# Perceiver layer on one core: block scales on GpSimd, early residual products, products of zeros on TensorE

## The chip, the cores and the metric

The kernel is one program on one core of one Trainium2 chip (trn2). The core has TensorE (PE), VectorE (DVE), ScalarE (ACT), GpSimd (POOL) and SyncE (SP), which run side by side and wait for each other by semaphores. The metric is the device time of one execution in microseconds. PEld is TensorE's weight load, which overlaps its products; PEclk is TensorE's granted clock as a share of full speed (1.00 is 2.4 GHz, 0.50 is 1.2 GHz).

## The reference

The layer takes x (4 x 256 x 256) and a context (4 x 4096 x 256), both f32, and adds three parts to x:

```python
x = x + xattn(layernorm(x), ctx, ctx)   # q, k, v products; focus (log, softmax, x mean) of q and k;
                                        # of 16 values in each head the 11 largest kept;
                                        # kv = k^T v per head; y = q kv / (q . mean k); y @ Wp.T
x = x + attn(layernorm(x))              # q * cumsum(k * v) * sigmoid(gate), with biases
x = x + ffn(layernorm(x))               # silu(gate) * up, then down: NVFP4 fake quantization of
                                        # rows, of the hidden rows and of the three weights
```

Fake quantization: every block of 16 values gets a scale, its absolute maximum / 6 times a global scale, limited to 448 and rounded to fp8 (e4m3); the values are divided by it and rounded to fp4 (e2m1). The global scale of a weight is 448 x 6 / (absolute maximum of the whole weight); that of the rows is an input (s_in, s_in_down).

## The kernel before, in words

Rows lie on the 128 partitions, and a group is 1024 rows: eight tiles of 128 rows by 256 columns. Group 0 is the query (x), groups 1 to 16 are the context. The order of each engine is written out by hand, and each engine's queue runs in that order; `wait_ge` holds up the engine and everything behind it in its queue.

**Start.** SyncE issues the loads: x in four parts, Wk, the first context group, gate_w, up_w, down_w, Wv, Wp. ScalarE's queue issues Wq. VectorE builds `ident` (`identity`), takes the statistics of x and writes the normalised rows `x_hat` (`query_rows`, L1238). TensorE transposes Wq (`transpose_quad(0, ...)`), then the query's rows (`query_turn`, L783), and multiplies (`project`, L811: eight products of 128x256 for two tiles). ScalarE moves each quad of transposes from PSUM to SBUF (`evacuate_quad`, L429) and lifts each product (`lift`, L482). VectorE takes between them the block maxima of the three weights of the feed-forward part (`weight_max`, L1268) as they land, and the sorting keys of the query's halves (`query_keys`, L1372). ScalarE's exponentials (L516) and VectorE's reciprocal of their sums (L1290) close group 0.

**Groups 1 to 16, in pairs.** VectorE makes keys (L1280), sorts them by a network of min and max (L1305 to L1356), makes the mask (L1363), and applies it (L1296). TensorE transposes, projects (L811) and sums k^T context (L908); ScalarE lifts, takes logarithms and exponentials and scales the rows (L528). Once the block maxima are there, GpSimd reduces their maximum over the partitions (L406, at 45.7 us).

**Attention.** Behind the last group: `mix` (products of q with kv, division on VectorE, L1449 to L1453), `mixed_quad` (transposes of the mixed rows, L783), `project_out` (L896), `add_attention`, statistics; then gates, running sums and, between them, the fp4 codes of the three weights (`scale_weight`, `weight_codes`). Between mix(1) and mix(2) VectorE's queue has `weight_scales` (L1507 to L1529: all scales of the feed-forward part, block scales rounded to fp8 in `w_fp8`, and `ident_out`, the identity times 1/out_scale); `weight_reciprocals` (L1534 to L1536) comes later.

**Feed-forward.** Four chunks of two tiles. TensorE: `gate_up` (L1029), `hidden_oct` (eight transposes of a tile's codes, L1039), `down`: the residual product `ident_out` x `xs` (L1049), then eight products with `downT` (L1052). ScalarE: `silu_half` (L671), `hidden_oct` (L679, one copy of 128x1024), `finish_rows` (L685) and `finish_tile` (L691). VectorE: `hidden` (L1483) and the quantization of the hidden rows, ending in L1214 for each tile. SyncE stores.

Of the kernel before, what the change touches and what calls it, by code (L numbers as in the profile page):

```python
# [18 lines left out]
P = 128  # L19
# [12 lines left out]
T = 8  # L32
# [32 lines left out]
def perceiver_layer(nc, x, ctx, Wq, Wk, Wv, Wp, focus, W_qkv, b_qkv, W_gate, b_gate,  # L65
# [9 lines left out]
    with es:  # L75
# [5 lines left out]
        oct_bank = bank[6:8]  # L81

# [87 lines left out]
        x_hat = expo[1]  # L170

# [36 lines left out]
        ident_ready = sem("ident_ready")  # L208
        w_rest_loaded = sem("w_rest_loaded")
# [10 lines left out]
        w_max_taken = sem("w_max_taken")  # L220
        front_loaded = [sem(f"front_loaded{s}") for s in range(PER_BATCH)]
# [52 lines left out]
        ident_out_ready = sem("ident_out_ready")  # L274
        down_in_psum = sem("down_in_psum")
# [6 lines left out]
        EVERY, LOWER, UPPER = slice(0, T), slice(0, T // 2), slice(T // 2, T)  # L282
        NORM_TILES = (LOWER, UPPER, LOWER, UPPER, LOWER, UPPER)
# [96 lines left out]
        def _(pool):  # L380
# [27 lines left out]


            pool.wait_ge(small_loaded, 64)  # L410
# [7 lines left out]
        def _(act):  # L418
# [203 lines left out]
            def spread_fp8(i, dst, fp8):  # L622

                act.wait_ge(fp8_rounded, max(i - 1, 1))
# [49 lines left out]
            def hidden_oct(t):  # L674
# [4 lines left out]
                act.activation(hid_fp4T[:, t % 2, :, :], oct_bank[t % 2][:, :].bitcast(BF16).rearrange("p (k c) -> p k c", k=8),  # L679
# [96 lines left out]
        def _(pe):  # L776
# [16 lines left out]

            pe.wait_ge(ident_ready, 4)
            pe.wait_ge(wq_loaded, 16)
            transpose_quad(0, two_tiles(w_rows, 0))

# [235 lines left out]
            def hidden_oct(t):  # L1033
# [3 lines left out]
                for b in range(8):  # L1037
                    at = (t % 2) * HIDDEN + b * P
                    ins = pe.transpose(oct_bank[t % 2][:, :].bitcast(BF16)[:, b * P:(b + 1) * P],  # L1039
                                       hid_fp4[:, at:at + P], ident_b[:, :])  # L1040
                ins.then_inc(oct_in_psum, 1)

            def down(t):

                c = t // 2
                dst = (bank[4] if t == T - 1 else bank[4 + c % 2])[:, (t % 2) * D:(t % 2 + 1) * D]
                if c >= 2:
                    pe.wait_ge(rows_out_ready, c - (t < T - 1))
                pe.matmul(dst, ident_out[:, :], xs[:, t, :], start=True, stop=False)  # L1049
                pe.wait_ge(oct_in_sbuf, FFN_OCTS + 2 + t + 1)  # L1050
                for k in range(HIDDEN // P):
                    ins = pe.matmul(dst, hid_fp4T[:, t % 2, k, :], downT[:, k, :], start=False, stop=(k == HIDDEN // P - 1))  # L1052
# [58 lines left out]
        def _(dve):  # L1111
# [108 lines left out]
            def identity():  # L1220

                step(dve.memset(ident[:, :], 0.0))
# [281 lines left out]
            each = lambda a: a[:, :].rearrange("p (w o) -> p w o", o=1).broadcast_to([P, 3, P])  # L1504
            flat_w = lambda a: a[:, :, :].rearrange("p w b -> p (w b)")

            def weight_scales():  # L1507

                dve.wait_ge(small_loaded, 64)
                dve.wait_ge(absmax_reduced, 1)  # L1510
                step(dve.reciprocal(in_scale_inv[:, :], in_scale[:, :]))
                then(dve.reciprocal(w_scale[:, :], w_absmax_all[:, :]))
                step(dve.tensor_scalar(in_sixth[:, :], in_scale[:, :], 1.0 / FP4_MAX, None, ALU.mult))
                then(dve.tensor_scalar(w_scale[:, :], w_scale[:, :], FP8_MAX * FP4_MAX, None, ALU.mult))
                step(dve.tensor_scalar(in_undo[:, :], in_scale_inv[:, :], NEARLY_ONE / HALF_WAY, None, ALU.mult))
# [184 lines left out]
```

## Time and profile before

| | |
|---|---|
| median of 3 runs | 482.53 us (481.84 to 482.94) |
| the profiled execution | 481.86 us, its span 480.1 us |
| busy VectorE, TensorE, ScalarE, GpSimd | 449.7, 383.1, 361.4, 7.4 us |
| granted clock of TensorE, mean | 0.947 |

The time of an execution is a little longer than its span, the stretch from the first to the last instruction in the record. In a row of the timeline stand the start in us, the duration in us, the engine, the line of the kernel, the operation, output<-input, the shape, how many instructions are merged (x8), and in brackets how long the engine had been idle before and what ended that. The end of a product on TensorE is modelled, and a group of products of which the ends overlap shows a little more than it occupies. In the chain, each row is start, length, engine, what, line.

### The profile page before, as it was taken

Reading aid. Unit: us, or ns where it says so; the run is one execution under the profiler, and the core shown is the slowest. Engines: PE = TensorE matmul, PEld = TensorE weight load, DVE = VectorE, ACT = ScalarE, POOL = GpSimd, SP = SyncE. Lnnn points to the kernel's source line nnn. Section 1 sums busy time; section 2 is a strip of 40 time slices with the busy share of each in tenths; the row PEclk is TensorE's granted clock in tenths of the full one; section 3 lists DMA queues with packets and bytes.
Section 4 is the critical chain, followed back from the end, with each engine's and each line's share of the span. In section 5 each row is a group of like instructions: output and inputs, shape, how many; then the busy total and the mean of one; then the engine's idle time right before and its main releaser. Section 6 shows DMA issues by size and latency. Waiting matters only on the chain.

```text
span 480.1 us, 5971 instructions
## 1 busy us (share of the span) xinstructions
PE 383.1 (80%) x1877; PEld 303.2 (63%) x1880; DVE 449.7 (94%) x706; ACT 361.4 (75%) x952; POOL 7.4 (2%) x22
## 2 busy tenths in 40 slices
PE   2996649998998988997897997991999789537764
PEld 1875537787776876886786885891885445213343
DVE  6699999999999999999999999999998879899993
ACT  2469986997997987997887988976438568666764
POOL 2001000000000000000000000000000000000000
PEclk9999879999999999999999999997899999958878
DMA  7933100230220230140140140041010000000001
GB/s 232 354 115 120 55 1 1 87 89 1 88 88 1 69 107 2 50 126 1 46 131 1 42 129 6 1 127 49 13 76 0 1 2 0 1 0 1 23 22 44
DMA packets 27070, 27.65 MB, mean 58 GB/s; under 512 B 1184, under 2 KB 26784, under 8 KB 27040
## 3 DMA queue, kind: packets, MB, share of 16 engines
q1 hardware_dynamic: 26464, 27.00, 17.9%
q8 instruction: 15, 0.25, 0.2%
q10 hardware_dynamic: 416, 0.26, 0.2%
q14 instruction: 15, 0.12, 0.1%
q0 software_dynamic: 160, 0.01, 0.0%
HBM read 26.22 MB, written 1.05 MB: 57 GB/s over the span
## 4 chain that ended last, share of the span: by engine, by line
DVE 73%; PE 9%; issue 9%; ACT 7%; DMA 1%; SPq 0%; ACTq 0%
DVE focus_words L1296 8%; DVE focus_words L1280 8%; DVE sorted L1319 4%; DVE level L1305 4%; DVE level L1306 4%; DVE sorted L1320 4%; DVE merge L1332 4%; PE bank L811 4%; DVE sorted L1197 3%; DVE amax L1166 2%; DVE sorted L1325 2%; DVE sorted L1324 2%; DVE keymax L1322 2%; DVE merge L1330 2%; DVE rank L1343 1%
## 5 line engine op out<-in xcount | busy, mean ns | idle before, releaser
L811 PE MATMUL bank<-WkT,rows_T 128*128 128x256 f32 x512 | 125.2, 391 | 33.5 <-ACT rows_T L429 33.5
L811 PEld LDWEIGHTS bank<-WkT,rows_T 128*128 128x128 f32 x512 | 95.3, 194 | 50.5 <-ACT rows_T L429 39.2
L908 PE MATMUL bank<-ctx_words,focus_words 128*128 128x257 f32 x512 | 115.3, 383 | 3.5 <-ACT focus_words L528 3.5
L908 PEld LDWEIGHTS bank<-ctx_words,focus_words 128*128 128x128 f32 x512 | 99.5, 197 | 16.1 <-ACT focus_words L528 5.5
L516 ACT ACTIVATE focus_words<-focus_words,shift,ff 128x256 f32<-128x256 f32 x136 | 79.8, 590 | 0.6
L482 ACT ACTIVATE focus_words<-bank 128x256 f32<-128x256 f32 x136 | 50.2, 381 | 28.8 <-PE bank L811 28.8
L528 ACT ACTIVATE focus_words<-focus_words,row_scale 128x256 f32<-128x256 f32 x136 | 56.2, 512 | 11.6 <-DVE row_scale L1298 11.6
L429 ACT ACTIVATE rows_T<-bank 128x512 f32<-128x512 f32 x78 | 44.2, 595 | 17.5 <-PE bank L783 17.5
L783 PE MATMUL bank<-ident,ctx_words 128*128 128x128 f32 x256 | 38.2, 278 | 3.5 <-DMA ctx_words<-in_ctx_dram 2.8
L1363 DVE TENSOR_TENSOR mask<-focus_words,fifth 128x2048 bf16<-128x2048 f32 x17 | 39.0, 2292 | 0.5
L783 PEld LDWEIGHTS bank<-ident,ctx_words 128*128 128x128 f32 x256 | 31.6, 144 | 11.5 <-DMA ctx_words<-in_ctx_dram 5.2
L1296 DVE TENSOR_TENSOR focus_words<-focus_words,mask 128x2048 f32<-128x2048 f32 x17 | 38.5, 2267 | 0.0
L1280 DVE SCALAR_TENSOR_TENSOR focus_words<-focus_words,key_and,key_xor 128x2048 int32<-128x2048 int32 x16 | 37.5, 2345 | 0.0
L499 ACT ACTIVATE focus_words<-focus_words 128x2048 f32<-128x2048 f32 x17 | 32.5, 1911 | 0.0
L993 PE MATMUL bank<-WattT,rows_T 128*128 128x512 f32 x64 | 29.4, 595 | 0.0
L482 ACT ACTIVATION_READ_ACCUMULATOR focus_words<-bank 128x1 f32 x136 | 27.9, 205 | 0.0
L1029 PE MATMUL bank<-gateT,focus_words 128*128 128x512 bf16 x29 | 11.6, 481 | 18.3 <-DVE ctx_words L1483 10.1
L516 ACT ACTIVATION_READ_ACCUMULATOR focus_words<-focus_words,shift,ff 128x1 f32 x136 | 25.7, 189 | 0.0
L1319 DVE TENSOR_TENSOR sorted<-level 128x1024 f32<-128x1024 f32 x17 | 20.8, 1224 | 0.5
L783 PE MATMUL bank<-ident,focus_words 128*128 128x128 f32 x64 | 11.4, 314 | 12.4 <-DMA focus_words<-in_L_xattn_Wq_dram 4.6
L1320 DVE TENSOR_TENSOR sorted<-level 128x1024 f32<-128x1024 f32 x17 | 20.7, 1218 | 0.0
L1332 DVE TENSOR_TENSOR merge<-sorted 128x1024 f32<-128x1024 f32 x17 | 20.7, 1217 | 0.0
(198 smaller groups left out, 584.1 us busy)
## 6 DMA issues: line engine op xcount, KB each, us to landing
ctx_words<-in_ctx_dram SPq DMA_DIRECT2D x32, 512.0 KB, 4.0
ctx_words<-in_L_ffn_gate_w_dram SPq DMA_DIRECT2D x2, 1024.0 KB, 8.4
ctx_words<-in_L_ffn_up_w_dram SPq DMA_DIRECT2D x2, 1024.0 KB, 9.3
xs<-in_x_dram SPq DMA_DIRECT2D x4, 256.0 KB, 5.6
ctx_words<-in_L_ffn_down_w_dram SPq DMA_DIRECT2D x2, 512.0 KB, 9.7
ctx_words<-in_L_ffn_down_w_dram SPq DMA_DIRECT2D x1, 1024.0 KB, 4.9
out_dram<-xs SPq DMA_DIRECT2D x3, 256.0 KB, 2.1
gateT<-in_L_attn_W_qkv_dram SPq DMA_DIRECT2D x1, 512.0 KB, 6.2
```

The costliest lines, as they stand in the source:

```text
L429: ins = act.activation(dst, src, ACT.Copy, scale=scale)
L482: ins = act.activation(lifted[(s + 1) % 2][:, t, :], proj_bank[m][:, (t % 2) * D:(t % 2 + 1) * D], ACT.Prelu, bias=NOT_ZERO, alpha=-0.01, ...
L516: ins = act.activation(expo[slot][:, t, :], lifted[slot][:, t, :], ACT.Exp, bias=shift[:, t:t + 1], scale=ff[:, 0:1], accum_out=exp_sum[:, ...
L528: ins = act.activation(expo[slot][:, t, :], expo[slot][:, t, :], ACT.Identity, scale=row_scale[:, slot, t:t + 1])
L783: ins = pe.transpose(quad_bank[par][:, b * P:(b + 1) * P], src, ident[:, :])
L811: ins = pe.matmul(proj_bank[m][:, t * D:(t + 1) * D], rows_T[:, m % 2, 2 * t + k, :], WT[:, k, :], start=(k == 0), stop=(k == KT - 1))
L908: ins = pe.matmul(sum_bank[k][:, 0:GW], heads_half(expo[slot][:, t, :], k), ctx_ring[:, s, t, :], start=(s == 0 and t == 0), stop=(s == PE ...
L1280: dve.scalar_tensor_tensor(out=key[n % 2].bitcast(I32), in0=lifted[(s + 1) % 2].bitcast(I32), scalar=key_and[:, 0:1], in1=key_xor[:, :].re ...
L1296: tt(expo[slot], expo[slot], mask[:, :, :], ALU.mult).then_inc(masked_ready, 1)
L1319: step(tt(sorted4[:, :, 2:4, :], level1[:, :, 0:2, :], level1[:, :, 2:4, :], ALU.max))
L1320: step(tt(sorted4[:, :, 0:5:4, :], level1[:, :, 0:2, :], level1[:, :, 2:4, :], ALU.min))
L1332: step(tt(low[:, at], sorted4[:, :, 0:4, 0:32], sorted4[:, :, 0:4, 32:64], ALU.min))
```

## The change

Four things are changed.

1. VectorE's `weight_scales` is taken apart. The four instructions with a reciprocal (or its factor) go into `tensor_scales`, in front of group 3's sorting. The other 13, and the first two of `weight_reciprocals`, run on GpSimd behind its all-reduce, each waiting for the one before by `pstep`; `out_undo` is a product there, not a reciprocal.
2. The residual product of `down` becomes `residual(t)`. For the even tiles it comes ahead of `hidden_oct`; for the last tile it comes between the two `hidden_oct` of the last chunk.
3. The last tile's transposes go half to their old bank and half to bank 0; ScalarE copies the first half, VectorE the second.
4. VectorE clears `zero_cols` (512 bf16 columns of `mask`) first of all, and TensorE multiplies them with themselves, 8 times ahead of Wq's transposes and 10 times behind, into a bank that is used later.

```diff
+        zero_cols = mask[:, 0:2, :].rearrange("p t c -> p (t c)")
...
+            pool.wait_ge(w_scale_ready, 1)
+            pool.tensor_scalar(in_sixth[:, :], in_scale[:, :], 1.0 / FP4_MAX, None, ALU.mult).then_inc(pstep, 1)
...
+            pool.wait_ge(pstep, 7)
+            pool.tensor_scalar(ident_out[:, :], ident[:, :], out_undo[:, 0:1], None, ALU.mult).then_inc(ident_out_ready, 1)
+            pool.tensor_tensor(w_amax[:, :, :], w_amax[:, :, :], each(w_sixth), ALU.mult).then_inc(pstep, 1)
+            pool.wait_ge(pstep, 8)
+            pool.tensor_scalar(w_amax[:, :, :], w_amax[:, :, :], FP8_MAX, None, ALU.min).then_inc(pstep, 1)
+            pool.wait_ge(pstep, 9)
+            pool.tensor_scalar(flat_w(w_magic), flat_w(w_amax), FP8_MAGIC, FP8_LEAST, ALU.mult, ALU.max).then_inc(pstep, 1)
+            pool.wait_ge(pstep, 10)
+            pool.tensor_tensor(flat_w(w_amax), flat_w(w_amax), flat_w(w_magic), ALU.add).then_inc(pstep, 1)
+            pool.wait_ge(pstep, 11)
+            pool.tensor_tensor(flat_w(w_fp8), flat_w(w_amax), flat_w(w_magic), ALU.subtract).then_inc(w_fp8_ready, 1)
+            pool.wait_ge(w_fp8_ready, 1)
+            pool.tensor_tensor(w_rcp[:, :, :], w_fp8[:, :, :], each(w_undo), ALU.mult).then_inc(pstep, 1)
+            pool.wait_ge(pstep, 12)
+            pool.tensor_scalar(w_rcp[:, :, :], w_rcp[:, :, :], TINY / HALF_WAY, None, ALU.max).then_inc(w_undone, 1)
...
+            blocks = slice(0, 4 if t == T - 1 else 8)
+            act.activation(hid_fp4T[:, t % 2, blocks, :], ...
...
+            def zero_products(n):
+                for _ in range(n):
+                    pe.matmul(sum_bank[1][:, :], zero_cols[:, 0:P], zero_cols, start=True, stop=True)
+            pe.wait_ge(zeros_ready, 1)
+            zero_products(8)
             pe.wait_ge(ident_ready, 4)
             pe.wait_ge(wq_loaded, 16)
             transpose_quad(0, two_tiles(w_rows, 0))
+            zero_products(10)
...
+            def residual(t):
                 c = t // 2
                 if c >= 2:
                     pe.wait_ge(rows_out_ready, c - (t < T - 1))
+                pe.matmul(down_dst(t), ident_out[:, :], xs[:, t, :], start=True, stop=False)
...
+                more = c + 1 < CHUNKS
+                residual(2 * c)
                 hidden_oct(2 * c)
+                if not more:
+                    residual(2 * c + 1)
                 hidden_oct(2 * c + 1)
                 down(2 * c)
+                if more:
+                    residual(2 * c + 1)
                 down(2 * c + 1)
...
+                dve.memset(zero_cols, 0.0).then_inc(zeros_ready, 1)
...
+            def tensor_scales():
+                dve.wait_ge(small_loaded, 64)
+                dve.wait_ge(absmax_reduced, 1)
+                step(dve.reciprocal(in_scale_inv[:, :], in_scale[:, :]))
+                then(dve.reciprocal(w_scale[:, :], w_absmax_all[:, :]))
+                then(dve.tensor_scalar(w_scale[:, :], w_scale[:, :], FP8_MAX * FP4_MAX, None, ALU.mult))
+                dve.reciprocal(w_scale_inv[:, :], w_scale[:, :]).then_inc(w_scale_ready, 1)
...
+                if a == 3:
+                    tensor_scales()
...
             def weight_reciprocals():
-                settle()
-                then(dve.tensor_tensor(w_rcp[:, :, :], w_fp8[:, :, :], each(w_undo), ALU.mult))
-                then(dve.tensor_scalar(w_rcp[:, :, :], w_rcp[:, :, :], TINY / HALF_WAY, None, ALU.max))
+                dve.wait_ge(w_undone, 1)
                 then(dve.reciprocal(w_rcp[:, :, :], w_rcp[:, :, :]))
...
             mix(0)
             mix(1)
-            weight_scales()
             mix(2)
...
+            dve.wait_ge(oct_in_psum, FFN_OCTS + 2 + T)
+            dve.tensor_copy(hid_fp4T[:, (T - 1) % 2, 4:8, :],
+                            last_half_bank[:, :].bitcast(BF16)[:, 0:4 * P].rearrange("p (k c) -> p k c", k=4))\
+                .then_inc(last_oct_half, 1)
```

## Rows read from the trace of the kernel before

**Rows 1.** The page's part 4: the chain that ended last, by engine.
```profile
DVE 73%; PE 9%; issue 9%; ACT 7%; DMA 1%; SPq 0%; ACTq 0%
```
**Rows 2.** Waits of VectorE: us in total, times, longest us.
```profile
DVE focus_words L1490 <- ACT ctx_words L652: 4.8, 4, 2.1
...
DVE rcp_sum L1290 <- ACT focus_words L516: 0.2, 1, 0.2
```
**Rows 3.** Timeline of the start, TensorE: the query's transposes and products.
```profile
9.85 1.97 PE L783 MATMUL bank<-ident,focus_words 128*128 128x128 f32 x8 [4.18 <-DVE focus_words L1238]
...
12.53 3.78 PE L811 MATMUL bank<-WqT,rows_T 128*128 128x256 f32 x8 [0.71 <-ACT rows_T L429]
...
16.96 2.69 PE L811 MATMUL bank<-WqT,rows_T 128*128 128x256 f32 x8
...
19.93 1.89 PE L811 MATMUL bank<-WqT,rows_T 128*128 128x256 f32 x8
```
**Rows 4.** Windows: PE, PEld, DVE, ACT, POOL busy (instructions), PEclk, DMA share, GB/s.
```profile
12.00:16.00 4.00, 3.47 (x8) 2.75 (x9) 2.40 (x10) 0.97 (x2) 0.51 (x2) 1.00 1.09 348
...
423.00:424.00 1.00, 1.00 (x4) 0.39 (x3) 1.00 (x2) 0.00 (x0) 0.00 (x0) 0.50 0.00 0
...
475.00:476.00 1.00, 1.00 (x6) 0.75 (x5) 0.00 (x0) 0.00 (x0) 0.00 (x0) 0.52 0.00 0
```
**Rows 5.** Timeline of the start, ScalarE and VectorE.
```profile
11.90 1.07 ACT L429 ACTIVATE rows_T<-bank 128x512 f32<-128x512 f32 x2
...
16.19 2.29 DVE L1268 TENSOR_REDUCE w_amax<-ctx_words 128x128 f32<-128x2048 f32 x1 [1.55 <-DMA ctx_words<-in_L_ffn_gate_w_dram]
...
20.56 1.28 DVE L1372 SCALAR_TENSOR_TENSOR focus_words<-focus_words,key_and,key_xor 128x1024 int32<-128x1024 int32 x1 [2.08 <-ACT focus_words L482]
```
**Rows 6.** Timeline, TensorE: bf16 products of 128x512 in the feed-forward part.
```profile
422.24 1.03 PE L1029 MATMUL bank<-gateT,focus_words 128*128 128x512 bf16 x2 [3.27 <-DVE ctx_words L1483]
423.06 1.06 PE L1029 MATMUL bank<-upT,focus_words 128*128 128x512 bf16 x2
```
**Rows 7.** DMA issues of the first 30 us: KB, median us to landing.
```profile
ctx_words<-in_L_ffn_up_w_dram SPq DMA_DIRECT2D x1, 1024.0 KB, 13.1
```
**Rows 8.** Windows of the two stretches on VectorE: length, busy (instructions), PEclk, DMA.
```profile
346.48:350.53 4.05, 3.77 (x18) 1.00 0.79 263
356.31:357.29 0.98, 0.91 (x3) 1.00 0.00 0
```
**Rows 9.** Timeline around weight_scales: ScalarE and TensorE.
```profile
343.98 3.30 ACT L528 ACTIVATE focus_words<-focus_words,row_scale 128x256 f32<-128x256 f32 x8 [6.83 <-DVE row_scale L1298]
...
347.82 3.72 PE L896 MATMUL bank<-WpT,rows_T 128*128 128x256 f32 x16 [0.19 <-ACT rows_T L429]
...
352.01 0.66 PE L783 MATMUL bank<-ident,focus_words 128*128 128x128 f32 x4 [0.47 <-DVE focus_words L1453]
```
**Rows 10.** Timeline: VectorE beside GpSimd's all-reduce, and one group later.
```profile
45.44 2.34 DVE L1280 SCALAR_TENSOR_TENSOR focus_words<-focus_words,key_and,key_xor 128x2048 int32<-128x2048 int32 x1
45.66 2.37 POOL L406 PARTITION_ALL_REDUCE w_absmax_all<-w_absmax  x1 [29.10 <-DVE w_absmax L1397]
47.82 1.23 DVE L1305 TENSOR_TENSOR level<-focus_words 128x1024 f32<-128x1024 f32 x1
...
56.16 2.34 DVE L1280 SCALAR_TENSOR_TENSOR focus_words<-focus_words,key_and,key_xor 128x2048 int32<-128x2048 int32 x1
```
**Rows 11.** The chain that ended last, behind VectorE's last code.
```profile
472.56 1.04 PE bank L1039 x8
473.59 0.96 PE bank L1049 x2
474.55 1.62 PE bank L1052 x8
...
476.61 0.89 PE bank L1052 x8
```
**Rows 12.** Timeline, TensorE: eight products of the second context group.
```profile
55.62 3.32 PE L811 MATMUL bank<-WkT,rows_T 128*128 128x256 f32 x8 [3.07 <-ACT rows_T L429]
```

More of the change, by code:

```diff
@@ L81, in perceiver_layer @@
         oct_bank = bank[6:8]
+        last_half_bank = bank[0]
         ctx_words = sb("ctx_words", [P, PER_BATCH * T * GW])
@@ L208, in perceiver_layer @@
         ident_ready = sem("ident_ready")
+        zeros_ready = sem("zeros_ready")
         w_rest_loaded = sem("w_rest_loaded")
@@ L220, in perceiver_layer @@
         w_max_taken = sem("w_max_taken")
+        w_scale_ready = sem("w_scale_ready")
+        pstep = sem("pstep")
+        w_fp8_ready = sem("w_fp8_ready")
+        w_undone = sem("w_undone")
         front_loaded = [sem(f"front_loaded{s}") for s in range(PER_BATCH)]
@@ L274, in perceiver_layer @@
         ident_out_ready = sem("ident_out_ready")
+        last_oct_half = sem("last_oct_half")
         down_in_psum = sem("down_in_psum")
@@ L282, in perceiver_layer @@
         EVERY, LOWER, UPPER = slice(0, T), slice(0, T // 2), slice(T // 2, T)
+        each = lambda a: a[:, :].rearrange("p (w o) -> p w o", o=1).broadcast_to([P, 3, P])
+        flat_w = lambda a: a[:, :, :].rearrange("p w b -> p (w b)")
         NORM_TILES = (LOWER, UPPER, LOWER, UPPER, LOWER, UPPER)
@@ L622, in spread_fp8 @@
             def spread_fp8(i, dst, fp8):
-                act.wait_ge(fp8_rounded, max(i - 1, 1))
+                if i < 3:
+                    act.wait_ge(w_fp8_ready, 1)
+                else:
+                    act.wait_ge(fp8_rounded, i - 2)
                 act.activation(dst.rearrange("p (b j) -> p b j", j=16),
@@ L678, in hidden_oct @@
                     act.wait_ge(down_in_psum, t - 1)
-                act.activation(hid_fp4T[:, t % 2, :, :], oct_bank[t % 2][:, :].bitcast(BF16).rearrange("p (k c) -> p k c", k=8),
+                blocks = slice(0, 4 if t == T - 1 else 8)
+                act.activation(hid_fp4T[:, t % 2, blocks, :],
+                               oct_bank[t % 2][:, :].bitcast(BF16).rearrange("p (k c) -> p k c", k=8)[:, blocks],
                                ACT.Copy).then_inc(oct_in_sbuf, 1)
@@ L1038, in hidden_oct, with down_dst, down @@
                     at = (t % 2) * HIDDEN + b * P
-                    ins = pe.transpose(oct_bank[t % 2][:, :].bitcast(BF16)[:, b * P:(b + 1) * P],
+                    dst, col = (last_half_bank, b - 4) if t == T - 1 and b >= 4 else (oct_bank[t % 2], b)
+                    ins = pe.transpose(dst[:, :].bitcast(BF16)[:, col * P:(col + 1) * P],
                                        hid_fp4[:, at:at + P], ident_b[:, :])
                 ins.then_inc(oct_in_psum, 1)
-            def down(t):
+            def down_dst(t):
+                return (bank[4] if t == T - 1 else bank[4 + t // 2 % 2])[:, (t % 2) * D:(t % 2 + 1) * D]
+            def residual(t):
                 c = t // 2
-                dst = (bank[4] if t == T - 1 else bank[4 + c % 2])[:, (t % 2) * D:(t % 2 + 1) * D]
                 if c >= 2:
                     pe.wait_ge(rows_out_ready, c - (t < T - 1))
-                pe.matmul(dst, ident_out[:, :], xs[:, t, :], start=True, stop=False)
+                pe.matmul(down_dst(t), ident_out[:, :], xs[:, t, :], start=True, stop=False)
+            def down(t):
                 pe.wait_ge(oct_in_sbuf, FFN_OCTS + 2 + t + 1)
                 for k in range(HIDDEN // P):
-                    ins = pe.matmul(dst, hid_fp4T[:, t % 2, k, :], downT[:, k, :], start=False, stop=(k == HIDDEN // P - 1))
+                    if t == T - 1 and k == 4:
+                        pe.wait_ge(last_oct_half, 1)
+                    ins = pe.matmul(down_dst(t), hid_fp4T[:, t % 2, k, :], downT[:, k, :], start=False,
+                                    stop=(k == HIDDEN // P - 1))
                 ins.then_inc(down_in_psum, 1)
```

33 lines of the change are left out of this document (9 added, 24 removed).

## Prediction

> **What bounds the kernel now.** I read the chain that ended last first, then VectorE's waits, then the timelines of both ends. The chain lies on VectorE for 73% of the span [rows 1], and VectorE's waits hold nothing of size between 43 and 334 us: a wait of 2.1 us for ScalarE's lift of the query at L1372 and one of 1.55 us for gate_w [rows 5], 0.2 us in all at L1290, and 4.8 us at the gates of the attention stage [rows 2]. So the run has three parts. Until 43 us VectorE waits for loads and for TensorE's first products. From 43 to 344 us VectorE alone decides, and what is put on it there is paid in full. Behind that TensorE and ScalarE hand work to each other until about 415 us; then VectorE decides again until its last instruction ends near 472.5 us, behind which only TensorE, ScalarE and a store are left.
>
> The profiled execution took 481.86 us, of which the span is 480.1; the median of the runs is 482.53. Every term below is a difference in the profiled execution; I add the sum to the median.
>
> **Products of zeros.** Between 12 and 16 us the granted clock is recorded as 1.00 [rows 4], yet eight of the query's products (128x256, f32) take 3.78 us from 12.53 us, 2.69 from 16.96 and 1.89 from 19.93 [rows 3]. The last is the rate of 2.4 GHz and the first is half of it: here the record does not show the low level and the durations do. The rate rose during the second eight, after TensorE had worked without a gap since 12.53 us; ahead of that it had done 12 transposes. The change gives it 8 products of 128x512 in bf16 from about 1.4 us, behind one memset, and 10 behind Wq's transposes. Two such products are 0.82 us apart at a granted clock of 0.50 [rows 6, 4], so one is 0.41 us at 1.2 GHz and half of that at 2.4. The eight last 3.3 us, to about 4.7; Wq's transposes, which ended 4.18 us ahead of 9.85 [rows 3], end some 0.3 us later, near 6.0. ScalarE has to take them out only in front of the query's rows, which it takes out at 11.90 us [rows 5]: no cost. The ten then take 2.1 to 4.1 us and end between 8 and 10.2; the query's transposes wait for x_hat until 9.85 us [rows 3], and a late end is hidden because ScalarE fetches them only at 11.90. The memset sits on VectorE in front of identity(), behind which VectorE waits for x anyway.
>
> If TensorE is then at 2.4 GHz from 12.53 us on, the first eight products take 1.9 us instead of 3.78 and the second eight 1.9 instead of 2.69, and the second lift is ready near 17.5 us, 3 us earlier. VectorE takes the first keys (L1372) at 20.56 us, having waited 2.08 us since its maximum of gate_w ended near 18.5 [rows 5]. That maximum began when gate_w had landed, at 16.19 us, and no faster TensorE moves it: of TensorE's 3 us VectorE gets the wait, and no more. Is another wait next? up_w, which the second maximum needs, lands 13.1 us behind its issue at 5.96 us [rows 7], at 19.1 us; VectorE would come to it after 19.8 at the earliest (18.5 and the 1.28 us of L1372). The 0.2 us at L1290 are for ScalarE's exponentials [rows 2], which follow TensorE's products and come forward with them. I take **-2.1 us**; bounds 0 (the rate falls back between 8 and 12.5 us, where TensorE has only eight transposes) and -2.3.
>
> **Block scales.** The two stretches that leave VectorE (L1511 to L1529, and L1534 with L1535) last 4.05 and 0.98 us [rows 8]. But that was not the path for all of it. The next step of TensorE that needs them to be over is the transposes of mixed rows 2, at 352.01 us; ahead of them in TensorE's queue stand two output projections, 347.82 to 351.54 us, which wait for ScalarE, and ScalarE scales the last rows from 343.98 to 347.28 us [rows 9]. With mix(2) on VectorE up to 4.05 us sooner, the transposes start at 351.5 instead of 352.0, and the last 32 products of the context, the third projection and ScalarE's evacuations behind them as much sooner; nothing in that chain is VectorE's. I take **-0.5 us**; bounds -0.3 and -1.2.
>
> What comes back to VectorE early: four small instructions in front of group 3, near 82 us. In the old stretch 17 instructions (the row counts one of mix(1) too) took 4.05 us [rows 8], 0.24 us each with the large among them; the four small ones, two of them followed by a settle, are at 0.14 us each some **+0.55 us**, all on the path (0.3 to 0.9).
>
> What GpSimd gets: 15 instructions, seven with 128x384 elements and one with 128x128. Nobody waits for them: their first user comes at 357 us, and what is queued behind them on GpSimd (the bias row's DMA, one memset) is far off too. Their price is what they do to VectorE beside them, and the trace has no such instruction. From below, 0: while GpSimd ran its all-reduce, from 45.66 us on, VectorE's L1280 took 2.34 us and L1305 followed 2.38 us behind its start; with GpSimd idle at 56.16 us L1280 took 2.34 too [rows 10]. But that instruction reads three elements of a partition, so it says little. From above: VectorE stands still for all of the moved work, which was 5.03 less 0.55, so **4.5 us**, on VectorE itself. I stay near the one row that shows both engines at once, take **+0.5 us** and keep both ends.
>
> The Trainium skill speaks against this part. "SBUF — State Buffer", section "Who interferes with whom", says that a VectorE instruction with two inputs in SBUF and a GpSimd instruction that reads SBUF block each other for a whole instruction; "GPSIMD Engine Reference", section 3.1, gives 1.96 times VectorE's duration for an addition. As an estimate from these two pages the cost would be 8.8 us and the sum below +5.7. The all-reduce's rows neither bear this out nor exclude it.
>
> **Residual products and the last tile.** In chunks 0 to 2 the residual moves to where TensorE waits for VectorE's codes, and VectorE, which decides there, waits for neither: 0. In the last chunk the path runs through TensorE from 472.56 us: eight transposes (1.04), tile 6's residual (0.96), its eight products (1.62), tile 7's residual, its eight products (0.89 from 476.61) [rows 11]. The change puts tile 6's residual into the idle stretch ahead of its transposes and tile 7's behind those, ahead of tile 7's; what it waits for there is ScalarE's rows of chunk 2, done before the first transposes are. Left are 1.04, 1.62 and tile 7's products, which begin at 475.2: the clock was at 0.50 until nearly 476 us [rows 4], so some four run at 1.2 GHz and four at 2.4, 1.25 us in all, to 476.45 instead of 477.50. That is **-1.05 us**; bounds -0.7 (all at 1.2 GHz) and -2.4 (the clock never falls). Halving the last evacuation adds nothing: ScalarE's whole copy would end before tile 6's products do.
>
> **Sum.** -2.1 - 0.5 + 0.55 + 0.5 - 1.05 = -2.6 us: 479.3 for the profiled execution, 479.9 at the median.
>
> **Rivals.**
> 1. The shared access: GpSimd's reads hold VectorE up for their whole length, where VectorE is the path. By rows 4.5 us in place of 0.5: 483.9 us, slower than before. For it: nearly every VectorE instruction near 82 us has two inputs in SBUF. Against it: the all-reduce's rows. It decides the sign once GpSimd costs VectorE over 3.1 us.
> 2. TensorE is not at 2.4 GHz at 12.53 us, as it does only eight transposes in the four microseconds before. For it: at 55.62 us, after 3.07 us of nothing, eight products took 3.32 us [rows 12]. The start then gives 0 to 0.7: 481.7 us.
> 3. The clock holds through the last tiles, -2.4 in place of -1.05: 478.5 us.
> 4. The start's gain meets another wait of VectorE before 43 us (a load, the exponentials) and 1 us of the 2.1 remains: 481.0 us.
>
> **How the numbers follow.** Forecast 479.9: 0.42, its own range 479.0 to 480.8. Rival 1, from half to the whole of its price: 0.25. Rival 2: 0.14. Rival 3: 0.09. Rival 4: 0.10. The range, 478.3 to 484.0, leaves out the far ends of rivals 1 and 3. Faster by over 0.2% (about what a measurement of this kernel can tell from no change), under 481.6: forecast, rivals 3 and 4, a third of rival 2, a little of rival 1: 0.67. Within 0.2%: the rest of rival 2 and the half-priced rival 1, 0.17. Slower: 0.16.
>
> **What would show it.** Right: eight products in 1.9 us at 12.5 us; no wait at L1372, and group 1's keys near 43.2 instead of 45.4 us; group 3 about 1 us longer; the transposes of mixed rows 2 right behind the projections; 1.0 us less between VectorE's last code and the end. Wrong: VectorE instructions near 82 us that last longer than their kind elsewhere (rival 1), 3.8 us for the first eight products (rival 2), a new wait of VectorE before 43 us (rival 4).

## The result, and the profile after

The changed kernel takes 483.75 us (median of 12 runs, 482.48 to 485.28), the kernel before, run beside it, 482.46 (12 runs). The ratio is 1.0027, interval 1.0015 to 1.0039: slower by 1.3 us, where 479.9 and faster was forecast. The time is inside the range, the direction is wrong. The profiled execution took 482.48 us, span 480.7, granted clock 0.939.

The two spans differ by 0.6 us only, less than the 1.3 us between the medians, because the profiled execution of the changed kernel is the fastest of its twelve. So the table below accounts for 0.6 us. To see where the time went, I read the start of the same VectorE instructions in both timelines: `row_scale(2)` is the last one ahead of the sorting of groups 3 and 4 ("pair 3" in the expectations), `row_scale(3)` comes behind their sorting, `row_scale(16)` is the last of the context.

| stretch | before | after | difference | predicted |
|---|---|---|---|---|
| start of the span to `row_scale(2)` | 84.66 | 83.87 | -0.8 | -2.1 |
| `row_scale(2)` to `row_scale(3)`: keys, sorting and mask of groups 3 and 4 | 29.98 | 33.29 | +3.3 | +0.55 and +0.5 |
| `row_scale(3)` to `row_scale(16)` | 229.1 | 229.1 | 0 | 0 |
| `row_scale(16)` to the end of the span | 136.4 | 134.4 | -2.0 | -0.5 and -1.05 |

The page of after: busy times, then the 40 slices of VectorE, GpSimd and the clock.

```profile
span 480.7 us, 6011 instructions
PE 388.8 (81%) x1895; PEld 305.2 (63%) x1898; DVE 449.4 (93%) x693; ACT 361.4 (75%) x952; POOL 27.6 (6%) x37
...
DVE  6799999999999999999999999999976869899994
...
POOL 3001000970000000000000000000000000000000
PEclk9898789998999999999999999997899999957988
```

VectorE has 13 instructions fewer and is busy only 0.3 us less (449.4 for 449.7), although some 5 us of work left it. GpSimd is busy 20.2 us more, in the eighth and ninth slice (84 to 108 us), where VectorE is full. That is the first thing that tells where the gain went. The timeline of VectorE there, in after (start, duration, engine, line, operation):

```profile
83.95 0.16 DVE L1483 RECIPROCAL in_scale_inv<-in_scale 128x2 f32<-128x2 f32 x1
...
84.51 1.20 DVE L1370 TENSOR_TENSOR level<-focus_words 128x1024 f32<-128x1024 f32 x1
85.63 1.22 DVE L1371 TENSOR_TENSOR level<-focus_words 128x1024 f32<-128x1024 f32 x1
...
92.84 2.37 DVE L1345 SCALAR_TENSOR_TENSOR focus_words<-focus_words,key_and,key_xor 128x2048 int32<-128x2048 int32 x1
95.24 1.73 DVE L1370 TENSOR_TENSOR level<-focus_words 128x1024 f32<-128x1024 f32 x1
96.90 1.52 DVE L1371 TENSOR_TENSOR level<-focus_words 128x1024 f32<-128x1024 f32 x1
98.45 1.41 DVE L1384 TENSOR_TENSOR sorted<-level 128x1024 f32<-128x1024 f32 x1
...
100.92 0.67 DVE L1387 TENSOR_REDUCE keymax<-sorted 128x8 f32<-128x512 f32 x1
...
102.24 1.40 DVE L1390 TENSOR_TENSOR sorted<-sorted 128x512 f32<-128x512 f32 x1
...
112.62 2.29 DVE L1428 TENSOR_TENSOR mask<-focus_words,fifth 128x2048 bf16<-128x2048 f32 x1
```

The same line takes 1.20 us at 84.51 and 1.73 us at 95.24; L1390 takes 1.40 us where its fellow of the first group takes 0.69. From the first sorting instruction to the mask it is 28.11 us, against 25.37 before (L1305 at 84.74 to L1363 at 110.11). The timeline of GpSimd in the same stretch of after:

```profile
84.79 1.01 POOL L421 TENSOR_SCALAR in_sixth<-in_scale 128x2 f32<-128x2 f32 x1 [37.56 <-DVE w_scale_inv L1486]
...
93.29 2.61 POOL L433 TENSOR_TENSOR w_amax<-w_amax,w_sixth 128x384 f32<-128x384 f32 x1
...
99.88 1.89 POOL L439 TENSOR_TENSOR w_amax<-w_amax,w_magic 128x384 f32<-128x384 f32 x1
...
104.41 1.56 POOL L445 TENSOR_SCALAR w_rcp<-w_rcp 128x384 f32<-128x384 f32 x1
```

GpSimd's instructions stand without a gap from 84.79 to 105.97 us, and the tensor_tensor at 93.29 takes 2.61 us. The timeline of TensorE's start in after, which answers [rows 3]:

```profile
1.25 3.60 PE L838 MATMUL bank<-mask 128*128 128x512 bf16 x8 [1.25 <-DVE mask L1286]
4.65 1.09 PE L824 MATMUL bank<-ident,focus_words 128*128 128x128 f32 x4
5.53 2.60 PE L838 MATMUL bank<-mask 128*128 128x512 bf16 x10
10.43 1.30 PE L824 MATMUL bank<-ident,focus_words 128*128 128x128 f32 x8 [2.31 <-DVE focus_words L1303]
13.12 3.56 PE L860 MATMUL bank<-WqT,rows_T 128*128 128x256 f32 x8 [1.38 <-ACT rows_T L465]
...
16.95 1.89 PE L860 MATMUL bank<-WqT,rows_T 128*128 128x256 f32 x8
```

The zeros did raise the rate: the ten behind Wq's transposes take 2.60 us where the eight ahead took 3.60, and the eight query transposes take 1.30 us instead of 1.97. But TensorE was empty for 2.31 us ahead of those and 1.38 behind, and the products at 13.12 us run at the low rate again, 3.56 us for eight (3.78 in [rows 3]). The record shows this fall. Windows of after, columns as in [rows 4]:

```profile
12.00:13.00 1.00, 0.00 (x0) 0.00 (x0) 0.79 (x9) 0.83 (x4) 0.00 (x0) 0.95 1.09 347
13.00:16.00 3.00, 2.88 (x7) 2.35 (x8) 2.13 (x9) 0.56 (x2) 0.00 (x0) 0.50 1.09 347
```

The granted clock is 1.00 until about 12.9 us, 0.50 from there to about 16.3 us, and 1.00 again behind that (these times, here and below, are estimates from the means of such windows). It is recorded as 1.00 too for the first eight zeros here and for the first products of before [rows 4], whose durations are those of the low level, so ahead of its first recorded fall the row can't be taken at its word. The second eight of the query's products, at 16.95 us, take 1.89 us instead of 2.69. That is not the zeros' doing: they take 1.89 us too in four kernels without zeros (e2, e4, e8_gpsimd_reads, e8_gpsimd_two_reads, all described below). The eight transposes that became 0.67 us shorter bring nothing by themselves: the first product follows their start by 2.69 us, before by 2.68, since it waits for ScalarE's copy.

The timeline of TensorE in after, in the attention stage, for [rows 9], and at the end, for [rows 11]:

```profile
350.37 3.72 PE L945 MATMUL bank<-WpT,rows_T 128*128 128x256 f32 x16 [0.52 <-ACT rows_T L465]
353.93 0.60 PE L824 MATMUL bank<-ident,focus_words 128*128 128x128 f32 x4
...
473.38 0.85 PE L1101 MATMUL bank<-xs,ident_out 128*128 128x256 f32 x2
474.45 1.03 PE L1089 MATMUL bank<-ident_b,ctx_words 128*128 128x128 bf16 x8 [0.22 <-DVE ctx_words L1278]
475.28 2.82 PE L1109 MATMUL bank<-downT,focus_words 128*128 128x256 bf16 x16
```

From `row_scale(16)` the transposes follow after 7.66 us (353.93 less 346.27), before after 8.29 (352.01 less 343.72): -0.63. They start right behind the sixteen projections ahead of them, where before TensorE was idle for 0.47 us [rows 9]. At the end, from the last transposes, it is 6.25 us to the end of the span, before 7.54 [rows 11]: -1.29.

### The profile page after: what moved, and what is told of

It is laid out like the page before. It is cut to its first block, busy times and chain, and to the rows that moved or that the text cites. A ratio compares the mean times of both kernels' runs of the same rounds, so it can differ in the third digit from the quotient of the medians.

```text
span 480.7 us, 6011 instructions
## 1 busy us (share of the span) xinstructions
PE 388.8 (81%) x1895; PEld 305.2 (63%) x1898; DVE 449.4 (93%) x693; ACT 361.4 (75%) x952; POOL 27.6 (6%) x37
## 3 DMA queue, kind: packets, MB, share of 16 engines
HBM read 26.22 MB, written 1.05 MB: 57 GB/s over the span
## 4 chain that ended last, share of the span: by engine, by line
DVE 71%; PE 10%; issue 10%; ACT 7%; DMA 1%; SPq 0%; ACTq 0%
DVE focus_words L1345 8%; DVE focus_words L1361 7%; DVE sorted L1384 4%; DVE level L1370 4%; DVE level L1371 4%; DVE merge L1397 4%; DVE sorted L1385 4%; PE bank L860 3%; DVE sorted L1261 3%; DVE amax L1230 2%; DVE sorted L1390 2%; DVE sorted L1389 2%; DVE keymax L1387 2%; DVE merge L1395 2%; DVE rank L1408 1%
## 5 line engine op out<-in xcount | busy, mean ns | idle before, releaser
L860 PE MATMUL bank<-WkT,rows_T 128*128 128x256 f32 x512 | 128.6, 399 | 34.3 <-ACT rows_T L465 34.3
L860 PEld LDWEIGHTS bank<-WkT,rows_T 128*128 128x128 f32 x512 | 97.9, 199 | 52.1 <-ACT rows_T L465 39.8
L710 ACT ACTIVATE ctx_words<-bank,out_scale 128x512 f32<-128x512 f32 x16 | 10.9, 686 | 13.1 <-PE bank L1078 11.9
```

Of the source, the lines that this page charges most:

```text
L860: ins = pe.matmul(proj_bank[m][:, t * D:(t + 1) * D], rows_T[:, m % 2, 2 * t + k, :], WT[:, k, :], start=(k == 0), stop=(k == KT - 1))
```

## The experiments

Theory A: GpSimd's reads of SBUF hold up VectorE's two-input instructions, about +2.7 us beside groups 3 and 4, and the zeros fail because TensorE falls back ahead of its first real products. Theory B: GpSimd costs VectorE nothing of size, and the loss comes from the other parts (the four instructions in front of group 3, the reordered residual, the zeros' memset). All runs in one table, each against executions of before that ran beside it (medians 482.29 to 482.46 us). The ratio is the one on record, and it differs from the ratio of the two medians by up to some 0.1%; the three columns on the right are from each profiled execution, the stretches of the table above (the one left out is 229.1 us in all of them).

| kernel | us (runs) | ratio, interval | to row_scale(2) | 2 to 3 | 16 to end |
|---|---|---|---|---|---|
| before | 482.29 to 482.46 | | 84.66 | 29.98 | 136.4 |
| after | 483.75 (12) | 1.0027, 1.0015 to 1.0039 | 83.87 | 33.29 | 134.4 |
| e1_scales_on_dve | 480.87 (11) | 0.9974, 0.9958 to 0.9989 | 85.30 | 29.99 | 135.5 |
| e2_scales_only | 484.67 (6) | 1.0047, 1.0031 to 1.0062 | 84.64 | 33.28 | 135.8 |
| e3_zeros_only | 482.53 (12) | 1.000, 0.998 to 1.002 | 83.87 | 29.99 | 137.6 |
| e4_residual_only | 480.86 (8) | 0.9965, 0.9948 to 0.9982 | 83.52 | 29.99 | 135.0 |
| e5_clock_held | 480.2 (7) | 0.9961, 0.9946 to 0.9976 | 82.95 | 29.98 | 136.5 |
| e10_no_six_zeros | 480.36 (10) | 0.9969, 0.9951 to 0.9986 | 82.94 | 29.98 | 136.1 |
| e7_scales_late | 479.76 (6) | 0.9948, 0.9932 to 0.9964 | 84.63 | 29.98 | 134.8 |
| e8_gpsimd_reads | 485.01 (4) | 1.0057, 1.0039 to 1.0075 | 84.11 | 33.74 | 135.8 |
| e8_gpsimd_writes | 482.27 (10) | 0.9989, 0.9972 to 1.0007 | 85.87 | 29.99 | 136.4 |
| e8_gpsimd_two_reads | 490.41 (4) | 1.0177, 1.0154 to 1.0199 | 83.92 | 38.33 | 136.4 |
| e9_late_and_held | 477.76 (5) | 0.9902, 0.9888 to 0.9916 | 82.36 | 29.99 | 134.8 |

The columns are not equally firm. "2 to 3" repeats to 0.01 us between kernels that do the same there. The start differs by itself, and so does the end: with the old end it is 136.4 in before, 137.6 in e3, 136.1 in e10. So a difference under 1 us in those columns is read from the instructions or left to the medians.

### The three parts of the change, one by one

**e1_scales_on_dve**: the kernel after with the scales back on VectorE, between mix(1) and mix(2); all 15 GpSimd instructions go.

```diff
-            pool.wait_ge(w_scale_ready, 1)
-            pool.tensor_scalar(in_sixth[:, :], in_scale[:, :], ...
...
-                if a == 3:
-                    tensor_scales()
...
+            weight_scales()
```

> The changed kernel with the block scales back on VectorE, at their old place; the zeros, the early residuals and the split last tile stay. Theory A (GpSimd's reads hold VectorE up in group 3): the profile of the changed kernel shows 2.7 us lost there and 0.56 us for the four instructions, against 0.6 won in the attention stage, so this kernel is 2.7 us faster than the changed one and 2.1 us faster than the kernel before (ratio 0.996). Theory B (GpSimd's work is harmless on average, the loss comes from the zeros or the new order at the end): about as long as the changed kernel, ratio 1.002 to 1.003. VectorE's instructions near 95 us last 1.22 us again under both.

Measured: 0.9974, a gain of 1.3 us by the ratio where theory A had 2.1; the interval still holds its 0.996 and shuts out theory B's 1.002. The scales alone turn a kernel that is 0.26% faster than before into one that is 0.27% slower. VectorE's durations beside groups 3 and 4 are back at those of before, timeline of e1:

```profile
93.70 2.35 DVE L1315 SCALAR_TENSOR_TENSOR focus_words<-focus_words,key_and,key_xor 128x2048 int32<-128x2048 int32 x1
96.09 1.23 DVE L1340 TENSOR_TENSOR level<-focus_words 128x1024 f32<-128x1024 f32 x1
97.23 1.22 DVE L1341 TENSOR_TENSOR level<-focus_words 128x1024 f32<-128x1024 f32 x1
```

**e2_scales_only**: the kernel before with the first part of the change alone, the whole GpSimd block.

```diff
+            pool.wait_ge(w_scale_ready, 1)
...
+                if a == 3:
+                    tensor_scales()
```

> The kernel before with the block scales moved to GpSimd and nothing else. Theory A: slower than before by 2.7 us, ratio 1.0056; VectorE's level instructions behind the second keys of pair 3 last 1.4 to 1.7 us instead of 1.22. Theory B: within 0.5 us of before.

Measured: 1.0047, and the stretch of groups 3 and 4 at 33.28 us, which is after's to 0.01. So the +3.3 us there needs neither the zeros nor the residual. The four instructions are in e2 as well, so what they cost is read from the trace: 0.56 us (83.95 to 84.51 in after). The other 2.7 are VectorE's longer instructions, and theory B falls.

**e3_zeros_only**: the kernel before with the zeros alone.

```diff
+                dve.memset(zero_cols, 0.0).then_inc(zeros_ready, 1)
...
+            pe.wait_ge(zeros_ready, 1)
+            zero_products(8)
             pe.wait_ge(ident_ready, 4)
             pe.wait_ge(wq_loaded, 16)
             transpose_quad(0, two_tiles(w_rows, 0))
+            zero_products(10)
```

> The kernel before with the products of zeros and nothing else. Theory A: 0.8 us faster (ratio 0.9983), the first eight query products still near 3.6 us as TensorE falls back to half its rate before them. Theory B: slower, because the zeros cost something that is not seen in one profile (x landing later), ratio 1.001 or more.

Measured: 1.000. This is neither theory A's 0.9983 nor theory B's 1.001 or more, and the interval (0.998 to 1.002) holds both: the zeros bring nothing that twelve executions can tell. The first eight products again stand at the low rate for nearly all their length. Timeline of TensorE, e3:

```profile
5.50 2.94 PE L799 MATMUL bank<-mask 128*128 128x512 bf16 x10
10.34 1.30 PE L785 MATMUL bank<-ident,focus_words 128*128 128x128 f32 x8 [1.90 <-DVE focus_words L1249]
13.02 3.28 PE L821 MATMUL bank<-WqT,rows_T 128*128 128x256 f32 x8 [1.38 <-ACT rows_T L431]
```

Windows of 0.5 and 1 us over these stretches show the granted clock fall to 0.50 in all three kernels with 8 and 10 zeros: from about 13.5 to 17.0 us in e3, from 12.9 to 16.3 in after, from 12.5 to 19.3 in e1. One execution of e3 took 477.99 us, the other eleven 482.13 to 484.48; it has no trace, so whether the clock held there is open.

The start of e3 and after (83.87 both, 85.30 in e1) has a mean of 84.35 us; the seven kernels without zeros (before, e2, e4, e7, the three e8) have 83.52 to 85.87, mean 84.48. After's -0.8 at the start is within that spread: it can't be called a gain of the zeros.

**e4_residual_only**: the kernel before with the residual and the last tile alone.

```diff
+                residual(2 * c)
                 hidden_oct(2 * c)
+                if not more:
+                    residual(2 * c + 1)
                 hidden_oct(2 * c + 1)
                 down(2 * c)
+                if more:
+                    residual(2 * c + 1)
```

> The kernel before with the early residual products and the split last tile and nothing else. Theory A: 1.3 us faster (ratio 0.9973), all of it behind VectorE's last code. Theory B: no gain, ratio 1.000.

Measured: 0.9965, -1.7 us by the ratio and -1.4 between the medians, near theory A's 1.3, and the only part of the change that pays as it stands. The product of the three ratios of e2, e3 and e4 is 1.0012, against 1.0027 for the change: the parts add up within the intervals.

### What GpSimd's access costs

Three kernels put 16 GpSimd instructions of 128x384 on the kernel before, beside the sorting of groups 3 and 4; besides them there is only a wait at `weight_scales`, 230 us later, for GpSimd to be done. Each writes `w_rcp`, which nobody uses yet; they do no work of the reference.

```diff
+            pool.wait_ge(row_scale_ready, 3)
+            for i in range(16):
+                if i:
+                    pool.wait_ge(ptest, i)
+                pool.tensor_scalar(w_rcp[:, :, :], w_amax[:, :, :], 1.0, None, ALU.mult).then_inc(ptest, 1)
```

In e8_gpsimd_writes the last line is `pool.memset(w_rcp[:, :, :], 1.0)`, in e8_gpsimd_two_reads a `tensor_tensor` with `w_amax` as both inputs.

> The kernel before, with 16 instructions added on GpSimd from group 2's row scale on (near 85 us), one behind the other: multiply w_amax (128x384, f32) by 1 into w_rcp, which is written anew later. They read and write SBUF. Theory A (reads of GpSimd exclude VectorE's instructions with two SBUF inputs): VectorE loses time in group 3, 16 times 0.3 to 0.5 us, so 5 to 8 us in all; ratio 1.010 to 1.017. Theory B (what cost time was the order or the waits, not the reads): no loss.

> The same 16 instructions at the same place as memsets of w_rcp (128x384, f32): they write as much and read nothing. Theory A as sharpened by the page on SBUF (only reads collide): no loss, ratio 1.000, VectorE's instructions near 90 us last 1.22 us. Theory C (any work of GpSimd costs VectorE): a loss like that with reads.

> Before, with 16 chained GpSimd tensor_tensor (128x384, two inputs, one output) beside the selection of pair 3, where e8_gpsimd_reads has 16 with one input. If VectorE loses time for each element that GpSimd reads: about twice the loss of e8_gpsimd_reads, 3.7 us in the trace's selection becomes 6 to 7.5, ratio 1.012 to 1.015. If it loses by GpSimd's busy time, whatever is read: as long as those are busy, and per us of GpSimd as in e8_gpsimd_reads (3.7 us for 26.7 us, 0.14). If it is the count of instructions: 1.0057 again.

The timelines show GpSimd's 16 instructions in one row. Of VectorE I show the second instruction of the sorting and, for two of the kernels, its reduction. First e8_gpsimd_writes:

```profile
86.16 7.55 POOL L416 MEMSET w_rcp<- 128x384 f32 x16 [36.92 <-DVE row_scale L1304]
...
87.08 1.22 DVE L1312 TENSOR_TENSOR level<-focus_words 128x1024 f32<-128x1024 f32 x1
```

The timeline of e8_gpsimd_reads:

```profile
84.47 26.68 POOL L416 TENSOR_SCALAR w_rcp<-w_amax 128x384 f32<-128x384 f32 x16 [36.99 <-DVE row_scale L1304]
...
85.33 1.52 DVE L1312 TENSOR_TENSOR level<-focus_words 128x1024 f32<-128x1024 f32 x1
...
89.66 0.67 DVE L1328 TENSOR_REDUCE keymax<-sorted 128x8 f32<-128x512 f32 x1
```

The timeline of e8_gpsimd_two_reads:

```profile
84.24 26.16 POOL L416 TENSOR_TENSOR w_rcp<-w_amax 128x384 f32<-128x384 f32 x16 [36.95 <-DVE row_scale L1304]
...
85.13 1.85 DVE L1312 TENSOR_TENSOR level<-focus_words 128x1024 f32<-128x1024 f32 x1
...
90.43 0.68 DVE L1328 TENSOR_REDUCE keymax<-sorted 128x8 f32<-128x512 f32 x1
```

The stretch takes 29.99 us beside the writes (nothing lost), 33.74 beside the one-input instructions (+3.8) and 38.33 beside the two-input ones (+8.4). GpSimd is busy about 26 us in both of the latter, and in both there are 16 instructions, so the loss goes neither by GpSimd's busy time nor by its count. It goes by what GpSimd reads: 0.23 us of VectorE's time for an instruction with one input of 384 elements, 0.52 us with two. The memsets are much shorter, 7.55 us in all, but at the one-input kernel's loss per busy us (3.75 / 26.68 = 0.14) they would have cost 1.1 us, and they cost none. Both expectations missed in size: one read cost 3.8 us and not 5 to 8, two reads 8.4 and not 6 to 7.5. VectorE's reduction, with one input, keeps its 0.67 us in all of them.

That prices the change itself. Its seven instructions of 128x384 are four with two inputs and three with one: 4 x 0.52 + 3 x 0.23 = 2.8 us; measured in after, 28.11 - 25.37 = 2.74. This is arithmetic after the fact, but its two prices come from other kernels. It leaves out `ident_out` (128x128), and it takes a scale that is spread over 128 blocks (the second input of two of the four) for a full input; no run tests either. The Trainium skill, "SBUF — State Buffer", section "Who interferes with whom", has the same rule: a VectorE instruction with two inputs in SBUF contends with a GpSimd instruction that reads there, one that only writes does not, and a reduction never does. The runs agree on which of the three GpSimd instructions collide and that the reduction does not; the last section has what does not fit so simply. They don't bear out the estimate of 8.8 us that the prediction worked out from that page and "GPSIMD Engine Reference", section 3.1: VectorE lost 2.74 us.

### The same scales elsewhere

**e7_scales_late**: e4 with the scales on GpSimd, but in the attention stage, where VectorE waits for others: `tensor_scales` stands between mix(1) and mix(2), and the GpSimd block is last in its queue.

```diff
+            tensor_scales()
...
             pool.memset(x_hat2[:, :, D - 1:D], 1.0).then_inc(ones_in_last, 1)
+            pool.wait_ge(w_scale_ready, 1)
```

> The early residuals and the split last tile as in e4, and the block scales on GpSimd, but in the attention stage: VectorE's four instructions between mix(1) and mix(2), GpSimd's 15 behind them, where VectorE's instructions have one input in PSUM or one input in all. No zeros. Theory A (only the place beside the sorting costs): 0.3 to 0.5 us faster than e4, ratio to before near 0.9957, and VectorE's instructions keep their durations. Theory B (GpSimd's work costs VectorE wherever it runs, or comes too late for the reciprocal at 357 us): 1 to 3 us slower than e4, ratio 0.999 to 1.003.

Measured: 0.9948, groups 3 and 4 back at 29.98 us. The timelines of GpSimd and VectorE in the attention stage of e7:

```profile
349.90 0.83 POOL L437 TENSOR_TENSOR w_amax<-w_amax,w_sixth 128x384 f32<-128x384 f32 x1
...
353.71 0.91 POOL L443 TENSOR_TENSOR w_amax<-w_amax,w_magic 128x384 f32<-128x384 f32 x1
...
356.61 1.17 POOL L449 TENSOR_SCALAR w_rcp<-w_rcp 128x384 f32<-128x384 f32 x1
...
353.96 0.68 DVE L1200 TENSOR_TENSOR rstd_a<-rstd 128x4 f32<-128x4 f32 x1 [0.30 <-ACT rstd L497]
...
357.81 2.55 DVE L1571 RECIPROCAL w_rcp<-w_rcp 128x384 f32<-128x384 f32 x1 [1.99 <-POOL w_rcp L449]
```

The same addition takes 0.91 us on GpSimd here and 1.89 beside the sorting in after: the hold-up works both ways. GpSimd's 15 instructions pass in 10.6 us (347.21 to 357.78) instead of 21.2. It isn't free: VectorE's tiny `rstd_a` takes 0.68 us instead of 0.16 (theory A had the durations unchanged), and its reciprocal now waits 1.99 us for GpSimd. Against e4 the stretch from `row_scale(16)` is only 0.2 us shorter, and the ratios (0.9948, 0.9965) overlap. So that the scales should leave VectorE at all is not shown; that they should not stand beside the sorting is.

### What held the clock

**e5_clock_held**: the kernel before with 8 zeros, then 20 instead of 10, and 6 more between the query's transposes and its first products. **e10_no_six_zeros**: the same without the 6.

```diff
             transpose_quad(0, two_tiles(w_rows, 0))
+            zero_products(20)
...
             query_turn(0)
             query_turn(1)
+            zero_products(6)
             project(0, 0, WqT)
```

> The kernel before with the zeros, but 20 instead of 10 behind Wq's transposes, and 6 more between the query's first eight transposes and its first product, so that TensorE has no stretch without products before 12.5 us. Theory A (the zeros were undone by the fall of the rate in the stretch from 8 to 12.5 us): the first eight query products take 1.9 us, VectorE does not wait at its first query keys, and the kernel is 1.5 to 2.1 us faster than before (ratio 0.9956 to 0.997). Theory B (the products' rate in the start does not decide, since x and gate_w land when they do): the products are fast and the time stays within 0.5 us of before.

> e5_clock_held without its last six products of zeros, so 8 and 20 remain and TensorE is empty between its transposes (end about 11.8) and the query's first products (13.2). If it is that last empty stretch that drops the rate: first eight at 3.3 to 3.8 us and the second eight at 1.9, ratio 0.998 to 1.000, as e3_zeros_only. If it was the empty stretch ahead of the transposes (8.1 to 10.4 in after) that mattered: first eight at 1.9 to 2.1 us, ratio 0.996.

Timeline of TensorE and of VectorE's first query keys, e10:

```profile
5.49 4.74 PE L799 MATMUL bank<-mask 128*128 128x512 bf16 x20
10.54 1.30 PE L785 MATMUL bank<-ident,focus_words 128*128 128x128 f32 x8 [0.31 <-DVE focus_words L1249]
13.22 1.99 PE L821 MATMUL bank<-WqT,rows_T 128*128 128x256 f32 x8 [1.38 <-ACT rows_T L431]
...
16.93 2.29 DVE L1279 TENSOR_REDUCE w_amax<-ctx_words 128x128 f32<-128x2048 f32 x1 [1.50 <-DMA ctx_words<-in_L_ffn_gate_w_dram]
19.13 1.28 DVE L1383 SCALAR_TENSOR_TENSOR focus_words<-focus_words,key_and,key_xor 128x1024 int32<-128x1024 int32 x1
```

With 20 zeros the empty stretch ahead of the query's transposes is 0.31 us (2.31 in after), the 1.38 us behind them is the same, and the first eight products take 1.99 us instead of 3.56. The granted clock, which fell to 0.50 in the three kernels with ten zeros there, is 1.00 from 12 to 17 us in e5, e10 and e9. So of the two empty stretches the first decided; the six zeros in the second neither help nor hurt (0.9961 and 0.9969, `row_scale(2)` at 82.95 and 82.94). The ten more zeros both fill the first stretch and add to TensorE's work ahead of it, and no run separates the two. The wait at the query's keys is gone, in after it is still 1.08 us. What is late next is gate_w, as the prediction had it: the maximum starts when it lands, at 16.93 us, and the keys follow at once. The gain of e5 is 1.9 us by the ratio (2.2 between the medians; e10: 1.5 and 2.0), and 1.7 us between the mean starts (82.75 for the three kernels that hold the clock, 84.48 for the seven without zeros).

### Both together

**e9_late_and_held**: the kernel after with the GpSimd block and `tensor_scales` placed as in e7, and the zeros as in e5.

> The kernel after with two of its parts moved: the scales' GpSimd block goes behind the last pair's preparation (as in e7_scales_late), and the zeros are 8, 20 and 6 more between the query's transposes and its first products (as in e5_clock_held). If the three parts act in stretches of their own, the ratios multiply: 0.9948 x 0.9961 = 0.991, some 478.2 us, with the first query products at 1.9 to 2.0 us and the selection's VectorE instructions at 1.22 us. If the start's gain and the attention's gain draw on the same slack (a later wait of VectorE takes one of them back), it is 0.9945 to 0.996, as either alone.

Measured: 477.76 us, 0.9902 (0.9888 to 0.9916), 4.7 us faster than before and 6 faster than after. The product of the ratios of e7 and e5 is 0.9909, so the two gains draw on different slack, as far as the intervals tell. VectorE's waits, e9 (us in total, times, longest), answering [rows 2]:

```profile
DVE focus_words L1566 <- ACT ctx_words L692: 4.8, 4, 2.1
DVE bn L1195 <- DMA xs<-in_x_dram: 2.7, 3, 1.6
DVE w_rcp L1583 <- POOL w_rcp L451: 2.0, 1, 2.0
```

No wait for the query's lift is in the list any more. The third row shows what is left to try: GpSimd's block would have to start 2 us earlier, and nothing here tried it.

## Why the prediction was wrong, by its steps

- **GpSimd beside VectorE, +0.5 us forecast, 2.74 measured.** This is the step that failed by most. The price was taken near the one row that showed both engines at once, the all-reduce beside L1280 [rows 10]. The prediction itself said that this row says little, and leaned on it all the same. Its VectorE side was fit: beside one and two reads of 384 elements that line goes from 2.35 to 2.58 and 2.91 us (e8_gpsimd_writes, reads, two_reads). Its GpSimd side was not: the all-reduce reads three elements of a partition. Rival 1 named the right mechanism and gave it 0.25 at half to the whole of 4.5 us; 2.74 is 0.6 of that. It said that the sign turns at 3.1 us, which holds for its own sum; with the zeros gone it turns near 1 us.
- **Zeros, -2.1 us forecast, no gain measured.** The failed step is "if TensorE is then at 2.4 GHz from 12.53 us on". TensorE was at 0.50 from 12.9 us on. The ten zeros ended at 8.1 us, where the prediction allowed 8 to 10.2 and called a late end harmless; it put no price on an early end, and with the zeros reaching to 10.2 us (e10) the clock held. Rival 2 had the fall, with 0.14, and put the start's gain at 0 to 0.7. The rest of the step held once the clock did: in e5 and e10 the products take 1.99 us, VectorE gains its wait and no more, and gate_w's landing is next.
- **Scales leaving VectorE, -0.5 forecast, -0.63 measured** at the transposes of mixed rows 2. Right, and for the reason given: VectorE waits 1.5 us there for the projection instead.
- **Four instructions in front of group 3, +0.55 forecast, +0.56 measured.** Right.
- **Residual and last tile, -1.05 forecast, -1.29 measured** in the two profiles, -1.7 by e4's ratio. Right in mechanism. From the last transposes to the end of the span the eight kernels with the old order take 6.93 to 8.75 us, mean 7.61, the five with the new one 5.97 to 6.65, mean 6.43: -1.2 us, so the forecast was close. The sixteen products behind the last transposes took 2.82 us in after, 2.45 in e4 and 3.25 in e7: the granted clock rises from 0.50 to 1.00 within them, at a point that differs between executions. Rival 3 (it never falls) did not come.
- **Rival 4** did not come: no new wait of VectorE ahead of 43 us took the start's gain in e5, e10 or e9.
- **The range** held the time, but by its width, not because the terms were right. Slower had 0.16. The forecast treated the two rivals that came as alternatives, while they come together. Rival 1's 2.2 us above the forecast's 0.5 and rival 2's 2.1 are 4.3 us, enough to turn -2.6 into +1.7; measured +1.3.

## What to carry to other kernels

Work that goes to GpSimd beside a saturated VectorE must not read SBUF while VectorE's two-input instructions run: here each GpSimd instruction with 384 elements cost VectorE 0.23 us with one input and 0.52 with two, and took up to three times its own time (2.61 us at 93.29 in after, 0.83 in e7). Put it where VectorE waits, and count the inputs it reads. Fillers that are to keep TensorE's clock up have to last until the next real work is near: the 10 products that ended 2.3 us ahead of the transposes bought nothing, 20 bought 1.5 to 1.9 us. Read both the durations of the products behind and the granted clock in short windows: the clock showed the fall at 12.9 us in after, but not the low level of the first products in the kernels without zeros.

## What the runs showed that was not expected

- GpSimd's seven small instructions (128x1 to 128x3) beside VectorE's sorting took 0.26 to 1.20 us each in after and 0.21 to 0.27 in e7, but VectorE kept its 1.22 us beside them. Only GpSimd pays for small reads there; VectorE pays from 95 us on.
- Not every two-input instruction of VectorE suffers alike. Beside the one-input GpSimd instructions L1312 went from 1.22 to 1.52 us, while L1330 (128x512) stayed at 0.68; beside the two-input ones L1331 went from 0.68 to 1.31 and L1330 to 0.71. Why is open: which one is hit may depend on which instruction came first, and no run separates that.
- VectorE's `rowmax` (a tensor_scalar of 128x8 with one more value for each partition, `key_flip`) is hit as well: 0.22 us in before, 0.46 beside the one-input instructions, 0.79 beside the two-input ones and in after. So the loss isn't confined to instructions with two whole tensors as inputs.
- The start of the query's transposes differs by over 1 us between executions of kernels with the same start (9.85 us in before, 11.01 in e8_gpsimd_writes). A profile of one execution can't tell a gain of 1 us there; the products' own durations can.
